# GpSimd's order inside a tile step: the low part of x behind h instead of in front of the class gather

## The chip, the core and the metric

The kernel runs on one core of a Trainium2 chip. The metric is the device time of one execution in microseconds (us), the median of several runs. The engines have names of their own here: PE is TensorE, ACT is ScalarE, DVE is VectorE, POOL is GpSimd, SP is SyncE, which issues transfers.

## What is computed

The input x has 2 batches of 2048 tokens with 512 features. A first layer adds a low-rank product with a decoded weight of each batch (rank 30). The second layer, whose cost rules the kernel, builds six variants of each token and runs an MLP with a layer norm over them:

```
x = x + x @ weight[b] + bias[b]                      # rank 30
h = ln(ln(x, pw_g[path], pw_b[path]), cp_g[comp], cp_b[comp])
t = ln(x, tm_g[comp], tm_b[comp]);   s = ln(x, ms_g[scale], ms_b[scale])
m, n, r = x + mlp_ln(state_k)                        # one vector each per batch
cat = [w0*h, w1*t, w2*m, w3*n, w4*r, w5*s]
x = x + ln(silu(cat @ W1 + b1) @ W2 + b2, g, be)
```

The products of cat that hold x itself are folded into one weight block, so that a tile needs four products of depth 512 in the first matmul (x, t, s, h) and one in the second.

## The kernel before

**Tiles and stages.** The 4096 tokens are 32 tiles of 128 tokens, tile number s. All engines run the same software pipeline: in step n, tile a = n+2 is loaded and embedded, f = n+1 gets its norms, m = n runs the first matmul, c = n-1 the second and b = n-2 the output norm. The order on every engine is written out by hand in a function `step(n)` of that engine; engines meet only at semaphores. Steps 15 to 26 are in a hardware loop of three rounds with four steps each (`steps`, `Fori`), the others are unrolled.

**Split operands.** Each float32 operand of a big product is split into a high part (fp32r) and a low part, and a product is three matmuls per chunk: high times high (L707), high times low (L708) and low times high (L709). 12 such matmuls of 128x512 make one product. For x the high part is made on ACT (`x_high`, L526) and the low part on POOL (`x_low`, L1034). For t, s, h and z the high part is ACT's copy (L555) and the low part a DVE subtraction that reads a PSUM bank (`split_lo`, L1210).

**Parked steps.** For tiles 2 to 13 the product with x was already computed in the preamble and parked in SBUF (`stash`). `kept(n)` says so: steps 2 to 13 have no x product, the other steps do ("unparked": 1 and 14 to 31). Only the unparked steps with a tile a to load, n = 1 and n = 14 to 29, are touched by the change.

**The chain of tile f on POOL and its neighbours.** In step n, PE's `expand(f)` (L768) ends with x1 on DVE (`first_sum`, L1242), then its statistics; POOL's `rstd(0, f)` turns them into rs and nm (L985, L993, L998); ACT makes xhat (`x_norm`, L604). From xhat, DVE makes st = xhat*sgt (`scale_rows`, L1262, needs the gather of sgt) and tt = xhat*ctt (`scaled`, L1254), then the low part of z of tile c (`z_split`, L1210 into zop), on which PE's `second_product(c)` (first matmul L707 that reads zop) waits, and then `out_scaled` (L1330). POOL makes h1 from xhat with two instructions (`h_first`: multiply L1043, add L1045; they need the gather of pwt). DVE takes its statistics (`h_stats`, L1215), POOL does `rstd(2, b)` and `rstd(1, f)`, ACT ht (`h_norm`, L611), DVE ht*ctt (`h_gain`, L1271) and then the low part of t (`t_split`); PE transposes ht at the start of the next step (`transpose_h`, L701) and then runs `t_product`.

**Gathers.** POOL issues three indirect transfers per tile a: ctt (`gather_class`, in the middle of the step; it also waits for tile a's indices and for `h_ready` of the tile whose slot it takes), and sgt and pwt (`gather_rest`, behind `rstd(1, f)`), all at L1010. The low part x_lo(a) is needed by PE's `embed(a)` (L758) near the end of the step and by the x product of the step n+2. The raw x of tile a comes by SP's queue (`load_x`), issued when PE has finished with the same slot.

Of the kernel before, what the change touches and what calls it, by code (L numbers as in the profile page):

```python
# [106 lines left out]
def kept(t):  # L107

    return t.i is None and PRE0 <= t.s < PRE0 + NPRE
# [13 lines left out]
def build(nc, d, out):  # L123
# [11 lines left out]
    with ExitStack() as ctx:  # L135
# [835 lines left out]
        def _(pool):  # L971
# [9 lines left out]
            def rstd(which, t, have, done):  # L981

                pool.wait_ge(have, t.count())
                pool.nop(nofuse=True)
                nc.gpsimd.tensor_scalar(ve[:, which:which + 1], mv[:, which, 1:2], EPS, 1.0, ALU.add, ALU.mult) \  # L985
                    .then_inc(pool_part, 1)
                parts[0] += 1
                pool.wait_ge(pool_part, part_count(t))
                if which == 2:
                    nc.gpsimd.tensor_tensor(rs[:, which:which + 1], ve[:, which:which + 1], mhalf[:, :],  # L990
                                            ALU.pow).then_inc(done, 1)
                    return
                nc.gpsimd.tensor_tensor(rs[:, which:which + 1], ve[:, which:which + 1], mhalf[:, :],  # L993
                                        ALU.pow).then_inc(pool_part, 1)
                parts[0] += 1
                pool.wait_ge(pool_part, part_count(t))
                pool.nop(nofuse=True)
                nc.gpsimd.tensor_scalar(nm[:, which:which + 1], mv[:, which, 0:1], rs[:, which:which + 1], -1.0,  # L998
                                        ALU.mult, ALU.mult).then_inc(done, 1)
# [14 lines left out]
            def gather_class(a):  # L1014
                s, old = a.slot, a.plus(-2)

                pool.wait_ge(idx_in[s], a.slot_count(16))
                if old.exists():
                    pool.wait_ge(h_ready, old.count())
                pool.nop(nofuse=True)  # L1020
                gather(a, ctt, "ct", 1, ct_in)

            def gather_rest(a):
                gather(a, sgt, "ms_g", 2, sg_in)
                gather(a, pwt, "pw", 0, pw_in)
# [5 lines left out]
            def x_low(a):  # L1031
                s = a.slot
                pool.wait_ge(x_hi, a.count())
                nc.gpsimd.tensor_tensor(xop[:, s, LO, :, :], xraw[s][:, :, :], xop[:, s, HI, :, :].bitcast(F32),  # L1034
                                        ALU.subtract).then_inc(x_lo, 1)

            def h_first(f):
                s = f.slot
                pool.wait_ge(xhat_ready, f.count())
                pool.wait_ge(pw_in[s], f.slot_count(16))  # L1040
                if f.plus(-1).exists():
                    pool.wait_ge(hn_ready, f.count(extra=0))
                nc.gpsimd.tensor_tensor(h1[:, :], xhat[:, :], pwt[:, s, 0:D], ALU.mult).then_inc(h1_part, 1)  # L1043
                pool.wait_ge(h1_part, f.count())
                nc.gpsimd.tensor_tensor(h1[:, :], h1[:, :], pwt[:, s, D:2 * D], ALU.add).then_inc(h1_ready, 1)  # L1045

            def residual(f):
                old = f.plus(-UNROLL)
                if old.exists():
                    pool.wait_ge(stored[f.row], old.row_count(16))  # L1050
                if is_first(f):
                    pool.wait_ge(bebc_in, 16)
                pool.wait_ge(x1_ready, f.count())
                nc.gpsimd.tensor_tensor(xb[:, f.row, :], x1[:, f.slot, :], bebc[:, :], ALU.add).then_inc(xb_ready, 1)  # L1054
# [23 lines left out]
            def step(n):  # L1078
                a, f, m, c, b = n.plus(2), n.plus(1), n, n.plus(-1), n.plus(-2)
                if f.exists():  # L1080
                    rstd(0, f, mv1_ready, r1_ready)
                if a.exists() and not kept(n):
                    x_low(a)
                if kept(n):
                    x_low(a)
                if a.exists():
                    gather_class(a)
                if f.exists():
                    h_first(f)
                if b.exists():  # L1090
                    rstd(2, b, mv3_ready, r3_ready)
                if f.exists():
                    rstd(1, f, mv2_ready, r2_ready)
                if a.exists():
                    gather_rest(a)
                if f.exists():
                    residual(f)

            first_step()
            for n in range(1, FIRST):  # L1100
                step(Tile(n))
            with pool.Fori(0, (LAST - FIRST) // UNROLL) as i:
                before = parts[0]
                base[:] = [20, i]
                for n in range(FIRST, FIRST + UNROLL):
                    step(Tile(n, i))
                assert parts[0] - before == 20
            parts[0] = before + 20 * ((LAST - FIRST) // UNROLL)
            base[1] = None
            for n in range(LAST, TILES):  # L1110
                step(Tile(n))
# [449 lines left out]
```

## Time and profile before

| what | value |
|---|---|
| time, median of 3 runs | 637.97 us (635.06 to 638.03) |
| the profiled execution's own time | 637.78 us |
| its span from first to last instruction | 636.0 us |
| busy: PE, PEld | 593.4 us, 453.1 us |
| busy: DVE, POOL, ACT | 407.6 us, 389.3 us, 204.9 us |
| mean granted TensorE clock | 0.992 of full speed |

The span is what the trace covers; the time adds 1.8 us around it. PEld is the weight load, which overlaps the matmul. A busy share is an average over stages with different limits, so it does not say by itself what a change in one stage does.

### The profile page before, as it was taken

The page shows a single profiled execution, that of the slowest core. Times are in us where ns is not written, and L with a number is a line of the kernel's source. Part 1 is how long each engine was busy: PE and PEld are TensorE (multiplying, and loading weights), DVE is VectorE, ACT ScalarE, POOL GpSimd, SP SyncE. Part 2 cuts the span into 40 slices and gives each one's busy share as a digit, 9 for nine tenths or more (in the row PEclk, how much of TensorE's full clock was granted, in tenths as well). Part 3 has the DMA queues.
Part 4 walks back from the last instruction along what each step waited for, and adds up shares of the span by engine and source line. Part 5 has one row for each costly group of instructions (what it writes and reads, how often), then busy time and mean ns, then how long its engine had stood idle before and what let it go on. Part 6 is the DMA issues. An engine that isn't in the chain of part 4 may idle for free.

```text
span 636.0 us, 9140 instructions
## 1 busy us (share of the span) xinstructions
PE 593.4 (93%) x2924; PEld 453.1 (71%) x2924; DVE 407.6 (64%) x749; ACT 204.9 (32%) x346; POOL 389.3 (61%) x499
## 2 busy tenths in 40 slices
PE   0899788989999999999999999999999999999995
PEld 0464245567878888888888777777888888787784
DVE  3411157658888888888865566556666565766655
ACT  3333235232333433334323323222333223323222
POOL 1013226666888888888856666676676676765820
PEclk9999799999999999999999999999999999999998
DMA  8999957513555445445524434444534344444301
GB/s 291 404 403 366 384 194 256 155 54 102 169 152 163 150 139 167 137 141 170 149 102 125 129 113 136 138 113 107 145 125 124 117 119 136 136 121 120 99 18 49
DMA packets 53119, 102.07 MB, mean 160 GB/s; under 512 B 10446, under 2 KB 23246, under 8 KB 52956
## 3 DMA queue, kind: packets, MB, share of 16 engines
q1 hardware_dynamic: 39872, 58.52, 27.0%
q0 software_dynamic: 12160, 42.04, 23.2%
q10 hardware_dynamic: 1052, 1.07, 0.5%
q8 instruction: 18, 0.29, 0.2%
q14 instruction: 17, 0.14, 0.1%
HBM read 93.10 MB, written 8.39 MB: 160 GB/s over the span
## 4 chain that ended last, share of the span: by engine, by line
PE 35%; POOL 16%; issue 12%; DVE 8%; DMA 8%; ACT 2%; POOLq 0%; DVEq 0%
PE bank L707 10%; PE bank L708 9%; PE bank L709 9%; DMA pwt<-in_pw,idx 7%; POOL h L1045 4%; PE bank L701 4%; POOL h L1043 3%; DVE bn L1215 3%; POOL rs L993 2%; POOL ctt L1010 2%; POOL ve L985 2%; POOL nm L998 1%; ACT ht L611 1%; DMA sgt<-in_ms_g,idx 1%; DVE x L1242 1%
## 5 line engine op out<-in xcount | busy, mean ns | idle before, releaser
L707 PE MATMUL bank<-W,ops 128*128 128x512 f32 x432 | 178.9, 414 | 1.3 <-DVE ops L1210 0.4
L708 PE MATMUL bank<-W,ops 128*128 128x512 f32 x432 | 171.3, 397 | 0.0
L709 PE MATMUL bank<-W,ops 128*128 128x512 f32 x432 | 171.0, 396 | 0.0
L707 PEld LDWEIGHTS bank<-W,ops 128*128 128x128 f32 x432 | 81.7, 189 | 29.7 <-issue 9.7
L555 ACT ACTIVATE ops<-bank 128x512 fp32r<-128x512 f32 x97 | 56.9, 589 | 136.8 <-PE bank L701 136.8
L709 PEld LDWEIGHTS bank<-W,ops 128*128 128x128 f32 x432 | 81.6, 189 | 20.0
L708 PEld LDWEIGHTS bank<-W,ops 128*128 128x128 f32 x432 | 81.9, 190 | 14.8
L1034 POOL TENSOR_TENSOR xop<-xraw,xop 128x512 fp32r<-128x512 f32 x32 | 41.8, 1307 | 65.9 <-ACT xop L526 65.8
L1210 DVE TENSOR_TENSOR ops<-bank,ops 128x512 fp32r<-128x512 f32 x97 | 66.2, 684 | 11.2 <-ACT ops L555 11.0
L1215 DVE BATCH_NORM_STATS2 bn<-h 128x6 f32<-128x512 f32 x32 | 22.2, 692 | 73.9 <-POOL h L1045 73.8
L985 POOL TENSOR_SCALAR ve<-mv 128x1 f32<-128x1 f32 x94 | 31.5, 336 | 39.5 <-DVE mv L1219 35.9
L604 ACT ACTIVATE xhat<-x,nm,rs 128x512 f32<-128x512 f32 x32 | 26.1, 815 | 83.7 <-POOL nm L998 83.7
L707 PE MATMUL bank<-W,zop 128*128 128x512 f32 x124 | 49.9, 402 | 2.1 <-DVE zop L1210 1.8
L1045 POOL TENSOR_TENSOR h<-h,pwt 128x512 f32<-128x512 f32 x32 | 48.4, 1513 | 2.5
L611 ACT ACTIVATE ht<-h,nm,rs 128x512 f32<-128x512 f32 x32 | 26.1, 815 | 73.5 <-POOL nm L998 73.5
L708 PE MATMUL bank<-W,zop 128*128 128x512 f32 x124 | 49.0, 395 | 0.0
L709 PE MATMUL bank<-W,zop 128*128 128x512 f32 x124 | 48.9, 394 | 0.0
L1010 POOL DMA_INDIRECT ctt<-in_ct,idx x32 | 37.8, 1181 | 15.9 <-DMA idx<-in_idx 8.0
L1043 POOL TENSOR_TENSOR h<-xhat,pwt 128x512 f32<-128x512 f32 x32 | 42.2, 1320 | 2.8 <-ACT xhat L604 1.2
L1054 POOL TENSOR_TENSOR xb<-x,bebc 128x512 f32<-128x512 f32 x32 | 42.1, 1317 | 0.6
L695 PE MATMUL bank<-ring,cst 128*32 128x480 f32 x128 | 19.0, 684 | 24.5 <-DMA ring<-in_W_dec 24.5
L1010 POOL DMA_INDIRECT sgt<-in_ms_g,idx x32 | 34.1, 1066 | 11.2 <-issue 11.2
(143 smaller groups left out, 1058.4 us busy)
## 6 DMA issues: line engine op xcount, KB each, us to landing
ring<-in_W_dec SPq DMA_DIRECT2D x16, 960.0 KB, 12.1
xraw<-in_xT SPq DMA_DIRECT2D x32, 256.0 KB, 4.8
x<-in_x SPq DMA_DIRECT2D x32, 256.0 KB
out<-xb SPq DMA_DIRECT2D x31, 256.0 KB, 2.0
ring<-in_int_W SPq DMA_DIRECT2D x4, 1024.0 KB, 13.4
mnr<-in_int_W SPq DMA_DIRECT2D x12, 256.0 KB, 8.2
stash<-in_xT SPq DMA_DIRECT2D x12, 256.0 KB, 12.1
idxrep<-in_rows SPq DMA_DIRECT2D x64, 32.0 KB, 4.8
```

The source lines that it names most:

```text
L555: nc.scalar.activation(dst.rearrange("p c t -> p (c t)"), bank[:, :], ACT.Copy).then_inc(done, 1)
L707: nc.tensor.matmul(bank[:, :], op[:, HI, c, :], w[:, HI, c, :], start=start and c == 0, stop=False)
L708: nc.tensor.matmul(bank[:, :], op[:, HI, c, :], w[:, LO, c, :], start=False, stop=False)
L709: last = nc.tensor.matmul(bank[:, :], op[:, LO, c, :], w[:, HI, c, :], start=False, stop=stop and c == KC - 1)
L985: nc.gpsimd.tensor_scalar(ve[:, which:which + 1], mv[:, which, 1:2], EPS, 1.0, ALU.add, ALU.mult) \
L1010: pool.indirect_dma_start(out=dst[:, s, :], out_offset=None, in_=d[table], in_offset=bass.IndirectOffsetOnAxis(ap=idx[:, s, col:col + 1], ...
L1034: nc.gpsimd.tensor_tensor(xop[:, s, LO, :, :], xraw[s][:, :, :], xop[:, s, HI, :, :].bitcast(F32), ALU.subtract).then_inc(x_lo, 1)
L1043: nc.gpsimd.tensor_tensor(h1[:, :], xhat[:, :], pwt[:, s, 0:D], ALU.mult).then_inc(h1_part, 1)
L1045: nc.gpsimd.tensor_tensor(h1[:, :], h1[:, :], pwt[:, s, D:2 * D], ALU.add).then_inc(h1_ready, 1)
L1054: nc.gpsimd.tensor_tensor(xb[:, f.row, :], x1[:, f.slot, :], bebc[:, :], ALU.add).then_inc(xb_ready, 1)
L1210: nc.vector.tensor_tensor(dst.rearrange("p c t -> p (c t)"), bank[:, :], hi.bitcast(F32).rearrange("p c t -> p (c t)"), ALU.subtract).then ...
L1215: nc.vector.bn_stats(bn[:, which, :], src).then_inc(bn_done, 1)
```

## The change

In POOL's `step(n)` the call `x_low(a)` of unparked steps stands behind `h_first(f)` instead of in front of `gather_class(a)`. Parked steps keep their order. Nothing else is touched; PE, DVE, ACT and SP have the same instructions in the same order.

```diff
                 if f.exists():
                     rstd(0, f, mv1_ready, r1_ready)
-                if a.exists() and not kept(n):
-                    x_low(a)
                 if kept(n):
                     x_low(a)
                 if a.exists():
                     gather_class(a)
                 if f.exists():
                     h_first(f)
+                if a.exists() and not kept(n):
+                    x_low(a)
                 if b.exists():
                     rstd(2, b, mv3_ready, r3_ready)
```

POOL's rows in step 1, the first unparked one, from the end of `rstd(0, f)` to the statistics of h. Before:

```order
48 L1034 TENSOR_TENSOR xop<-xraw_77,xop 128x512
49 L1010 DMA ctt<-in_ct,idx 128x1024
50 L1043 TENSOR_TENSOR h_90<-xhat,pwt 128x512
51 L1045 TENSOR_TENSOR h_90<-h_90,pwt 128x512
52 L985 TENSOR_SCALAR ve<-mv 128x1
```

And of the changed kernel:

```order
48 L1010 DMA ctt<-in_ct,idx 128x1024
49 L1043 TENSOR_TENSOR h_90<-xhat,pwt 128x512
50 L1045 TENSOR_TENSOR h_90<-h_90,pwt 128x512
51 L1034 TENSOR_TENSOR xop<-xraw_77,xop 128x512
52 L985 TENSOR_SCALAR ve<-mv 128x1
```

The subtraction into xop moved past one gather and two instructions of h; the row behind it is where it was.

In the hardware loop, POOL's rows of the first step of a round, with the semaphores that each waits for. Before:

```order
262 L998 TENSOR_SCALAR nm_97<-mv_94,rs_96 128x1 [waits pool_part]
263 L1033 REGISTER_ALU
264 L1034 TENSOR_TENSOR xop_75<-xraw1_77,xop_75 128x512 [waits x_hi]
265 L1017 ISA
266 L1019 REGISTER_ALU [waits idx_in1]
267 L1010 DMA ctt_81<-in_ct,idx_73 128x1024 [waits h_ready]
268 L1043 TENSOR_TENSOR h1_90<-xhat_87,pwt_83 128x512 [waits hn_ready,pw_in0,xhat_ready]
269 L1045 TENSOR_TENSOR h1_90<-h1_90,pwt_83 128x512 [waits h1_part]
```

And of the changed kernel:

```order
262 L998 TENSOR_SCALAR nm_97<-mv_94,rs_96 128x1 [waits pool_part]
263 L1017 ISA
264 L1019 REGISTER_ALU [waits idx_in1]
265 L1010 DMA ctt_81<-in_ct,idx_73 128x1024 [waits h_ready]
266 L1043 TENSOR_TENSOR h1_90<-xhat_87,pwt_83 128x512 [waits hn_ready,pw_in0,xhat_ready]
267 L1045 TENSOR_TENSOR h1_90<-h1_90,pwt_83 128x512 [waits h1_part]
268 L1033 REGISTER_ALU
269 L1034 TENSOR_TENSOR xop_75<-xraw1_77,xop_75 128x512 [waits x_hi]
```

The wait for x_hi, which stood ahead of gather and h, now stands behind both.

## Rows read from the trace of the kernel before

**Rows 1.** Step windows, expand to expand: length, each engine's busy us, clock, DMA.
```profile
319.05:335.96 16.91, 16.91 (x84) 13.93 (x83) 12.09 (x22) 5.71 (x10) 10.32 (x14) 1.00 0.33 112
...
405.84:423.89 18.05, 17.20 (x84) 13.84 (x83) 10.07 (x20) 4.79 (x9) 11.09 (x15) 1.00 0.39 114
...
sum 276.57, PE 274.30 PEld 222.09 DVE 173.93 ACT 82.29 POOL 183.36; mean PE 17.14 PEld 13.88 DVE 10.87 ACT 5.14 POOL 11.46
```

**Rows 2.** Waits from 319 to 606 us: us in total, times, longest.
```profile
POOL xop L1034 <- ACT xop L526: 54.5, 16, 4.7
...
DVE st L1262 <- DMA sgt<-in_ms_g,idx: 9.1, 7, 1.9
...
PEld bank L707 <- DVE zop L1210: 3.4, 5, 1.0
...
PEld bank L701 <- DVE ht L1271: 2.1, 5, 0.6
```

**Rows 3.** Timeline of a long step (expand at 405.84): start, us, instruction, [idle before].
```profile
411.77 0.69 DVE L1262 TENSOR_TENSOR st<-xhat,sgt 128x512 f32<-128x512 f32 x1 [1.90 <-DMA sgt<-in_ms_g,idx]
...
413.80 0.49 PE L707 MATMUL bank<-W,zop 128*128 128x512 f32 x1 [0.85 <-DVE zop L1210]
...
414.33 1.29 POOL L1034 TENSOR_TENSOR xop<-xraw,xop 128x512 fp32r<-128x512 f32 x1 [4.73 <-ACT xop L526]
...
418.20 1.29 POOL L1045 TENSOR_TENSOR h<-h,pwt 128x512 f32<-128x512 f32 x1
...
422.77 1.05 POOL L1010 DMA_INDIRECT sgt<-in_ms_g,idx  x1 [0.33 <-issue]
```

**Rows 4.** Timeline of a short step (expand at 319.05).
```profile
319.49 0.69 DVE L1242 TENSOR_TENSOR x<-bank,x 128x512 f32<-128x512 f32 x1 [2.66 <-PE bank L768]
...
322.37 0.26 POOL L998 TENSOR_SCALAR nm<-mv,rs 128x1 f32<-128x1 f32 x1 [0.18 <-POOL rs L993]
...
324.12 0.69 DVE L1254 TENSOR_TENSOR tt<-xhat,ctt 128x512 f32<-128x512 f32 x1
...
325.08 1.29 POOL L1034 TENSOR_TENSOR xop<-xraw,xop 128x512 fp32r<-128x512 f32 x1 [2.45 <-ACT xop L526]
...
325.99 0.39 PE L707 MATMUL bank<-W,zop 128*128 128x512 f32 x1
...
329.90 0.40 PE L758 MATMUL bank<-xop,Ust 128*128 128x256 f32 x2
```

**Rows 5.** Transfers issued from 319 to 590 us: KB each, median us to landing.
```profile
pwt<-in_pw,idx POOLq DMA_INDIRECT x15, 6.5
```

**Rows 6.** Timeline of the preamble: a class gather right behind rstd.
```profile
91.94 0.27 POOL L998 TENSOR_SCALAR nm<-mv,rs 128x1 f32<-128x1 f32 x1 [0.18 <-POOL rs L993]
...
92.67 1.07 POOL L1010 DMA_INDIRECT ctt<-in_ct,idx  x1 [0.46 <-issue]
```

**Rows 7.** Timeline of step 30 (expand at 595.62), which has no x_low and no gather.
```profile
596.70 0.68 DVE L1242 TENSOR_TENSOR x<-bank,x 128x512 f32<-128x512 f32 x1
...
600.71 0.69 DVE L1262 TENSOR_TENSOR st<-xhat,sgt 128x512 f32<-128x512 f32 x1 [0.69 <-ACT xhat L604]
601.00 1.55 POOL L1043 TENSOR_TENSOR h<-xhat,pwt 128x512 f32<-128x512 f32 x1 [1.17 <-ACT xhat L604]
...
601.32 1.78 DVE L1254 TENSOR_TENSOR tt<-xhat,ctt 128x512 f32<-128x512 f32 x1
...
603.75 0.50 PE L707 MATMUL bank<-W,zop 128*128 128x512 f32 x1 [0.60 <-DVE zop L1210]
```

**Rows 8.** Timeline at 516 us: POOL asks 0.16 us after DVE.
```profile
516.25 0.74 DVE L1330 SCALAR_TENSOR_TENSOR o<-o,mv,gbc 128x512 f32<-128x512 f32 x1
516.41 1.74 POOL L1034 TENSOR_TENSOR xop<-xraw,xop 128x512 fp32r<-128x512 f32 x1 [2.85 <-ACT xop L526]
```

**Rows 9.** Timeline of the first step of a loop round (expand at 475.76).
```profile
479.25 0.26 POOL L998 TENSOR_SCALAR nm<-mv,rs 128x1 f32<-128x1 f32 x1 [0.18 <-POOL rs L993]
...
481.25 0.68 DVE L1254 TENSOR_TENSOR tt<-xhat,ctt 128x512 f32<-128x512 f32 x1
```

## The prediction

> **What bounds the kernel now.** I read the windows of the 16 unparked steps 14 to 29 first, each from one `expand` on PE to the next. The reader is to see that a step is as long as PE is busy in the short one (16.91 of 16.91 us), while the longest takes 18.05 with PE busy for 17.20, and that the 16 sum to 276.57 [rows 1]. The clock is full. So 16.9 us is PE's own work, and 276.57 - 16 x 16.9 = 6.2 us is PE late in small pieces. Nothing else in these steps can be won, whatever moves on POOL.
>
> Then the chain of waits, for what PE stands still for: the low part of z (zop) and ht [rows 2]. Behind them stand DVE's wait for the gather of sgt, 9.1 us in 7 steps, and POOL's wait for x_hi in front of `x_low`, 54.5 us in all 16 [rows 2].
>
> Last the timeline of a long step. `x_low` starts at 414.33 after POOL has stood idle for 4.73 us, because the raw x lands late and ACT's copy with it; h ends at 419.49 and sgt's gather goes out at 422.77, 16.9 us after the step's expand [rows 3]. In the short step that idle time is only 2.45 us [rows 4]. Late gathers are felt one step on: sgt kept DVE waiting 1.90 us here and PE 0.85 us [rows 3]. It is a ring: late gathers crowd the raw x, which makes `x_low`, h and the next gathers late.
>
> **The change, part by part.** No instruction is added or removed. In steps 14 to 29 the order after `rstd(0)` was x_low, ctt, multiply, add; now it is ctt, multiply, add, x_low. I count times from the step's `expand`, with the short step as the pattern: x1 starts at 0.44, `rstd(0)` ends at 3.58, tt starts at 5.07, PE's first matmul of `second_product` at 6.94, `embed` at 10.85 [rows 4]. st ends 0.08 after tt starts [rows 7], at 5.15.
>
> *Gather.* Behind rstd a class gather started 0.46 us after nm and took 1.07 us [rows 6]. So it runs 4.04 to 5.11, and the multiply can start at 5.15 (0.04 us behind the gather, as in every step). It asks for pwt: issued at about 14.3 of the step before (below) and with a median of 6.5 us to landing [rows 5], that is 20.8 - 16.9 = 3.9, in time.
>
> *h and x_low.* If DVE keeps its pace, tt, 0.69 us long, holds the multiply up until 5.76 - 0.14: a POOL instruction that waits for a DVE one goes on 0.14 us before that one's end (the multiply behind st ended at 602.55, which is 601.40 - 0.14 + 1.29) [rows 7]. Multiply ends at 6.9. `out_scaled` (0.74 us [rows 8]) goes between, and the add ends at 8.6. `x_low` follows, 1.29 us long [rows 4], from 8.7 to 10.0, now after x_hi in nearly every step, so its wait for x_hi is gone. `embed` at 10.85 asks for it: 0.85 us to spare. Cover gone, each later us would be a us of the step.
>
> *What comes earlier.* From h's end to sgt's issue it was 3.28 us, with both rstd between [rows 3]; 0.25 of it was a wait for the statistics of h, which are now done before. So sgt goes out at 10.0 + 3.0 = 13.0 and pwt (1.05 us and 0.3 of issue later) at 14.3, where sgt went out at 16.9 in the long step [rows 3]. So the sgt wait of DVE disappears, and ht and the low part of t, which hang on the same `rstd(1)`, come 2 to 4 us earlier, more than PE ever waited for them. All the pieces of the 6.2 us go. The ctt gather goes out 4 to 6 us earlier and has the raw x beside it only at its end; I cost that at nothing, since ACT's copy of the raw x now has until 8.7 where it was needed at 6.0 [rows 4].
>
> *Step 30* starts x1 1.08 us after its expand, held up by late ht and t splits [rows 7], against 0.44 [rows 4]. So its zop and PE come 0.64 us earlier. Together 6.8 us.
>
> *The price.* h now runs beside st and tt. Rows 7 are that case: the multiply asks at 601.00, while st runs; when st ends, POOL goes first, and tt takes 1.78 us in place of 0.69. The trace shows one waiting for the other for a whole instruction: tt ends at multiply's end - 0.14 + 0.69. PE then starts zop's product late. PE starts 0.65 us behind tt's end [rows 7]. For a short step: st ends at 5.15, multiply at 5.15 - 0.14 + 1.29 = 6.30, tt at 6.85, PE at 7.50 in place of 6.94: **0.56 us** per step. Who is first decides. Where POOL asked 0.16 us after DVE had begun, DVE went first and POOL took 1.74 us [rows 8]. In an ordinary step the multiply asks at 5.15 and tt begins at 5.07, so DVE is first by 0.08 us and the price is 0. In the first step of each loop round (three of them: 15, 19, 23) tt begins 1.74 us behind rstd's end [rows 9] and the multiply asks 0.46 + 1.07 + 0.04 = 1.57 behind it: POOL is first. There tt would begin at 5.49, 0.42 later than in the pattern, so PE starts at 7.92: 0.98 us, three times 2.9 us.
>
> The bounds of that price: 0 where DVE is first everywhere; 13 x 0.56 + 2.9 = 10.2 us where POOL is first everywhere. I take DVE first in ordinary steps, by 0.08 us, which is thin: with a gather 0.33 us behind nm, as sgt's is [rows 3], it would turn.
>
> On who waits, the Trainium skill (SBUF — State Buffer, "A bandwidth-pool intuition that's wrong") says of GpSimd and a two-port instruction of VectorE that "one fully blocks"; GPSIMD Engine Reference, "Specifications", counts VectorE instructions with two SBUF inputs among those that contend. The trace agrees: tt 1.78 us in place of 0.69 [rows 7]. By the rule alone, without the order of asking, every step would pay, and the sum would be that of the second case below.
>
> *Step 1* changes too: h of tile 2 comes some 2 us earlier, but DVE is in long weight splits then; 0, within 1 us either way.
>
> **The sum.** 637.78 (the profiled execution, 0.2 under the median) - 6.8 + 2.9 = **633.9 us**, 0.6% faster.
>
> **Rivals.**
> 1. *No stall at all* (DVE first in the loop's first steps too): 637.78 - 6.8 = 631.0. For it: the margin there is 0.17 us, and the instructions between nm and the gather may take longer in the loop. Chance 0.13.
> 2. *POOL first everywhere; slower.* Then 6.8 is won and 10.2 paid: 641.2 us. It decides where the multiply asks before 5.07, that is, where the gather starts less than 0.38 us behind nm. For it: sgt starts 0.33 behind nm [rows 3]. Against it: 0.46 in the only sample of ctt [rows 6], and one more semaphore is waited for here. Chance 0.23.
> 3. *Mixed:* the winner changes from step to step, half of the 13 steps pay: 637.6. Also where some of the late landings stay, since the transfers' crowd only moves. Chance 0.14.
> 4. *x_low becomes late for embed.* Its wait replaces the one removed. It begins where h ends after 9.4, so with pwt landing after 6. With sgt issued at 13.0 it would need 8.6 us to land, against a median of 6.5 [rows 5]. Price, if it lasts at 0.3 us over: 16 x 0.3 = 4.8, with the rest 638.7; at 0.6 us over 643.5. Chance 0.07.
> My own case, DVE first but in the loop's first steps, has 0.43.
>
> **How the numbers follow.** The likeliest case gives 633.9; its own range is 632.5 to 635.5. Case 1 lies below, 2 and 3 above. From 630.5 to 641.5 lie all but case 4's upper part and the tails. A measurement here tells about 0.5% (3.2 us) from no change. Faster by more than that, under 634.8: case 1 and most of my own, 0.50. Slower, over 641.2: half of case 2 and half of case 4 with tails, 0.17. Between: 0.33.
>
> **What would show it.** Right: step windows of 16.9 us outside the loop's first steps and 17.9 in these; no wait of DVE for sgt; no wait of PE for ht; sgt issued near 13 us after expand; `x_low` ending about 10.0, `embed` not waiting; L1254 0.69 us long in ordinary steps and the multiply 1.7 to 1.8. If L1254 takes 1.78 in ordinary steps and the windows are 17.5, case 2 holds. The prediction is wrong in its base if windows stay uneven with sgt landing late, or if PE waits for xop before `embed`.

## The result, and the profile after

The change makes the kernel slower: 657.49 us (656.43 to 657.99, 6 runs) against 638.00 us of the kernel before (6 runs), ratio 1.0307, 95% interval 1.0283 to 1.0332. The forecast was 633.9 us with a range of 630.5 to 641.5.

The profiled execution took 657.37 us, 655.6 of it span. The windows from expand to expand, as in [rows 1], of the changed kernel: length, busy us of each engine, granted clock, DMA share, GB/s. The last row is steps 14 to 29 in one.

```profile
320.41:338.15 17.74, 17.20 (x85) 13.85 (x84) 12.89 (x22) 5.72 (x10) 12.20 (x15) 1.00 0.42 129
338.15:359.49 21.34, 18.73 (x84) 15.05 (x83) 14.92 (x21) 5.06 (x9) 12.40 (x15) 0.92 0.41 123
359.49:377.29 17.80, 17.20 (x84) 13.86 (x83) 12.34 (x21) 5.20 (x9) 12.07 (x15) 1.00 0.35 94
412.99:434.31 21.32, 18.73 (x84) 14.98 (x83) 14.91 (x21) 5.06 (x9) 12.40 (x15) 0.92 0.44 125
487.80:509.09 21.29, 18.70 (x84) 14.97 (x83) 14.92 (x21) 5.06 (x9) 12.40 (x15) 0.92 0.38 121
320.41:615.81 295.40, 279.80 (x1329) 225.11 (x1328) 205.34 (x337) 81.95 (x145) 195.46 (x240) 0.98 0.39 118
```

The 16 steps take 295.40 us where they took 276.57 [rows 1]: 18.8 of the 19.6 us between the two spans. The unevenness is gone, as forecast, but the ordinary steps are equally long at 17.7 to 17.9, not 16.9, and the first step of each loop round takes 21.3. The waits between 319 and 625 us (us in total, times, longest) show where PE stands:

```profile
DVE ops L1210 <- ACT ops L555: 17.7, 16, 3.0
PE bank L707 <- DVE zop L1210: 16.0, 17, 2.6
PEld bank L707 <- DVE zop L1210: 14.3, 14, 1.1
```

The waits for sgt and for ht of [rows 2] no longer stand among them; the one for zop has grown. The timeline of an ordinary step (expand at 359.49), on POOL, DVE and PE:

```profile
362.80 0.26 POOL L998 TENSOR_SCALAR nm<-mv,rs 128x1 f32<-128x1 f32 x1 [0.18 <-POOL rs L993]
...
363.61 1.03 POOL L1010 DMA_INDIRECT ctt<-in_ct,idx  x1 [0.54 <-issue]
...
363.94 0.69 DVE L1262 TENSOR_TENSOR st<-xhat,sgt 128x512 f32<-128x512 f32 x1 [0.69 <-ACT xhat L604]
364.55 1.98 DVE L1254 TENSOR_TENSOR tt<-xhat,ctt 128x512 f32<-128x512 f32 x1
364.67 1.30 POOL L1043 TENSOR_TENSOR h<-xhat,pwt 128x512 f32<-128x512 f32 x1
...
367.18 0.50 PE L707 MATMUL bank<-W,zop 128*128 128x512 f32 x1 [0.60 <-DVE zop L1210]
```

Gather and multiply start where they were put: 4.12 and 5.18 us behind expand (forecast 4.04 and 5.15); tt begins at 5.06. But tt takes 1.98 us and ends at 7.04, while the multiply, recorded 0.12 us behind it, takes 1.30, as if alone. PE starts zop's product at 7.69 in place of 6.94 [rows 4]. And the first step of a round (expand at 338.15):

```profile
342.52 1.03 POOL L1010 DMA_INDIRECT ctt<-in_ct,idx  x1 [0.61 <-issue]
...
343.04 2.41 DVE L1262 TENSOR_TENSOR st<-xhat,sgt 128x512 f32<-128x512 f32 x1 [0.84 <-ACT xhat L604]
...
343.59 1.30 POOL L1043 TENSOR_TENSOR h<-xhat,pwt 128x512 f32<-128x512 f32 x1
...
344.96 1.60 POOL L1045 TENSOR_TENSOR h<-h,pwt 128x512 f32<-128x512 f32 x1
345.37 1.74 DVE L1254 TENSOR_TENSOR tt<-xhat,ctt 128x512 f32<-128x512 f32 x1
...
347.84 0.79 PE L707 MATMUL bank<-W,zop 128*128 128x512 f32 x1 [2.61 <-DVE zop L1210]
```

Here st itself takes 2.41 us, though it begins 0.55 us before the multiply; then tt loses against the add. PE stands still for 2.61 us, and behind that the granted clock falls to half for 3.4 us of the step, in each of the three. The windows of the stall, of the stretch behind it and of the next 3.7 us show it (the clock is the third number from the end):

```profile
345.24:347.84 2.60, 0.00 (x0) 0.00 (x1) 2.60 (x4) 0.00 (x0) 2.60 (x2) 1.00 0.27 109
347.84:351.28 3.44, 3.44 (x8) 2.76 (x9) 3.03 (x5) 0.00 (x0) 2.23 (x5) 0.50 0.02 5
351.28:355.00 3.72, 3.72 (x23) 3.21 (x23) 0.97 (x3) 1.54 (x3) 2.84 (x5) 1.00 0.52 166
```

### The profile page after: what moved, and what is told of

The parts are those of the page before. It is cut to its first block, busy times and chain, and to the rows that moved or that the text cites. A ratio compares the mean times of both kernels' runs of the same rounds, so it can differ in the third digit from the quotient of the medians.

```text
span 655.6 us, 9140 instructions
## 1 busy us (share of the span) xinstructions
PE 600.4 (92%) x2924; PEld 458.3 (70%) x2924; DVE 439.2 (67%) x749; ACT 204.2 (31%) x346; POOL 396.4 (60%) x499
## 4 chain that ended last, share of the span: by engine, by line
PE 58%; DVE 13%; issue 4%; ACT 3%; POOL 3%; POOLq 0%; DVEq 0%; ACTq 0%
PE bank L707 16%; PE bank L708 15%; PE bank L709 15%; PE bank L701 6%; DVE tt L1254 5%; ACT xhat L604 2%; DVE bn L1215 2%; PE bank L758 2%; DVE x L1242 2%; POOL rs L993 2%; DVE zop L1210 2%; PE bank L777 1%; PE bank L768 1%; POOL nm L998 1%; POOL ve L985 1%
## 5 line engine op out<-in xcount | busy, mean ns | idle before, releaser
L985 POOL TENSOR_SCALAR ve<-mv 128x1 f32<-128x1 f32 x94 | 26.5, 281 | 98.9 <-DVE mv L1219 94.0
L707 PE MATMUL bank<-W,zop 128*128 128x512 f32 x124 | 52.8, 426 | 16.0 <-DVE zop L1210 16.0
L1034 POOL TENSOR_TENSOR xop<-xraw,xop 128x512 fp32r<-128x512 f32 x32 | 48.5, 1515 | 11.0 <-ACT xop L526 10.9
L1242 DVE TENSOR_TENSOR x<-bank,x 128x512 f32<-128x512 f32 x32 | 22.0, 688 | 47.5 <-PE bank L768 47.5
L1045 POOL TENSOR_TENSOR h<-h,pwt 128x512 f32<-128x512 f32 x32 | 51.1, 1598 | 2.5
L708 PE MATMUL bank<-W,zop 128*128 128x512 f32 x124 | 50.8, 410 | 0.0
L709 PE MATMUL bank<-W,zop 128*128 128x512 f32 x124 | 50.7, 409 | 0.0
L1254 DVE TENSOR_TENSOR tt<-xhat,ctt 128x512 f32<-128x512 f32 x32 | 43.5, 1360 | 2.3 <-ACT xhat L604 2.3
L707 PEld LDWEIGHTS bank<-W,zop 128*128 128x128 f32 x124 | 24.5, 197 | 29.3 <-DVE zop L1210 14.5
L993 POOL TENSOR_TENSOR rs<-ve,mhalf 128x1 f32<-128x1 f32 x64 | 40.2, 629 | 5.5 <-POOL ve L985 0.2
```

Of the source, the lines that this page charges most:

```text
L707: nc.tensor.matmul(bank[:, :], op[:, HI, c, :], w[:, HI, c, :], start=start and c == 0, stop=False)
L708: nc.tensor.matmul(bank[:, :], op[:, HI, c, :], w[:, LO, c, :], start=False, stop=False)
L709: last = nc.tensor.matmul(bank[:, :], op[:, LO, c, :], w[:, HI, c, :], start=False, stop=stop and c == KC - 1)
L1254: nc.vector.tensor_tensor(tt[:, :], xhat[:, :], ctt[:, s, D:2 * D], ALU.mult).then_inc(t_ready, 1)
```

## The experiments

Two theories. **P**: h's multiply on GpSimd takes the SBUF access that st and tt on DVE need; the low part of z is late, and PE waits. **T**: the class gather, 3.4 to 5.9 us earlier, hurts by its transfers. Each run is compared with the kernel before on the same chip. That one's median was 638.12 us (25 runs) for four of them (h held until tt, the early gather alone, the gather behind h, the low part of z first) and 637.69 us (23 runs) for the other four.

**Hold h back until tt is done.** In `h_first` of the changed kernel:

```diff
+                if f.s >= 15:
+                    pool.wait_ge(t_ready, f.count())
                 nc.gpsimd.tensor_tensor(h1[:, :], xhat[:, :], pwt[:, s, 0:D], ALU.mult)
```

> The changed kernel, but from step 14 on h's multiply also waits for tt (t_ready), so that it can't come between st and tt. Theory P (GpSimd's multiply takes the SBUF access that tt needs, so the low part of z and PE's second product are late): tt takes 0.69 us again, PE does not wait for zop, ordinary steps take 16.9 us, the whole about 631 us. Rival T (the class gather, 4 to 6 us earlier, hurts by its transfers): nothing of that kind changes, 655 us or more. In the first steps of the loop's rounds, where st took 2.4 us: if the multiply queued behind the gather is what blocks st, st takes 0.69 us and the step 16.9; if the gather itself blocks it, st takes about 1.2 us and the step over 17.2.

632.77 us, ratio 0.992 (0.9889 to 0.995): 0.8% faster than the kernel before, 3.8% than the changed one. One window over the 16 steps, and the first step of a round (expand at 404.56; two lines more in the file, so st is L1264, tt L1256 and the multiply L1045):

```profile
319.91:590.75 270.84, 270.84 (x1329) 222.59 (x1328) 183.36 (x337) 83.16 (x145) 185.63 (x240) 1.00 0.42 127
```

```profile
408.93 1.02 POOL L1010 DMA_INDIRECT ctt<-in_ct,idx  x1 [0.60 <-issue]
409.46 0.69 DVE L1264 TENSOR_TENSOR st<-xhat,sgt 128x512 f32<-128x512 f32 x1 [0.86 <-ACT xhat L604]
410.07 0.69 DVE L1256 TENSOR_TENSOR tt<-xhat,ctt 128x512 f32<-128x512 f32 x1
...
410.94 1.29 POOL L1045 TENSOR_TENSOR h<-xhat,pwt 128x512 f32<-128x512 f32 x1 [0.98 <-DVE tt L1256]
```

PE is busy for all 270.84 us, 16.93 a step. P holds, T falls: the gather is as early as in the changed kernel and costs nothing. In the first step of the round the gather started 0.60 us behind nm and st 0.53 behind the gather, just as in the slow one, and st takes 0.69 us. So it is not the gather that keeps st out, but the multiply queued behind it.

**Hold h back until st is done.** The same line with `s_ready`.

> The changed kernel, but h's multiply waits for st (s_ready) and not for tt: it can ask only once st is done and tt has begun. If an instruction that has the access keeps it, tt takes 0.69 us, the multiply about 1.6, steps 16.9, and the whole is as with the wait for tt, 632 to 633 us. If GpSimd goes first whenever it asks, tt takes 1.8 us or more and the whole 645 us or more.

632.84 us, ratio 0.9919 (0.989 to 0.9948). The multiply now asks 0.26 us behind tt's start and waits itself (expand at 355.03):

```profile
360.11 0.68 DVE L1256 TENSOR_TENSOR tt<-xhat,ctt 128x512 f32<-128x512 f32 x1
360.37 1.58 POOL L1045 TENSOR_TENSOR h<-xhat,pwt 128x512 f32<-128x512 f32 x1 [0.19 <-DVE st L1264]
```

So GpSimd does not go first whenever it asks; whoever has the access keeps it for the instruction. With 0.12 us behind tt and its waits met during the gather the multiply was first, with 0.26 and a wait met only at st's end it was second.

**The early gather alone.**

```diff
                 if a.exists():
                     gather_class(a)
+                if a.exists() and not kept(n):
+                    x_low(a)
                 if f.exists():
                     h_first(f)
-                if a.exists() and not kept(n):
-                    x_low(a)
```

> The class gather is in front, but x_low stays ahead of h: order gather, x_low, h. P: st and tt have nothing beside them, since x_low waits for the high part of x; L1254 0.69 us; time that of the kernel before, 638 us within 3. T: the early gather alone costs, 645 us or more.

633.12 us, ratio 0.9913 (0.9885 to 0.9941). Better than either theory had it: T is refuted a second time, but the 638 us given for P failed too, since that figure left out what the earlier gather wins. The same window, and the first step of a round (expand at 405.25):

```profile
320.60:591.46 270.86, 270.86 (x1330) 222.57 (x1329) 183.51 (x337) 82.06 (x145) 189.77 (x240) 1.00 0.42 127
```

```profile
409.62 1.02 POOL L1010 DMA_INDIRECT ctt<-in_ct,idx  x1 [0.60 <-issue]
410.15 0.69 DVE L1262 TENSOR_TENSOR st<-xhat,sgt 128x512 f32<-128x512 f32 x1 [0.86 <-ACT xhat L604]
...
411.61 1.29 POOL L1034 TENSOR_TENSOR xop<-xraw,xop 128x512 fp32r<-128x512 f32 x1 [0.96 <-ACT xop L526]
```

All that could be won in these steps comes from moving the gather ahead of `x_low`'s wait; that h also moved brought nothing. Behind the gather now stands an instruction whose wait (x_hi) is not yet met, and st passes with the same 0.53 us distance. POOL's wait in front of `x_low` is at most 1.3 us, where it was up to 4.7 [rows 2].

**The gather behind h.**

```diff
-                if a.exists():
+                if a.exists() and kept(n):
                     gather_class(a)
                 if f.exists():
                     h_first(f)
                 if a.exists() and not kept(n):
+                    gather_class(a)
                     x_low(a)
```

> The class gather behind h too: order rstd, h, gather, x_low. P, as step 30 of the kernel before: the multiply asks while st runs, tt takes 1.8 us, PE starts zop's product 0.56 us late and loses 0.7 us a step in all, also in the first steps of the rounds (1.0 to 1.3 there), 642 to 644 us. If only the gather makes the trouble (T, or a gather that holds the access itself): 631 to 638 us.

645.30 us, ratio 1.0111 (1.0078 to 1.0144), 1.3 us over the expected 642 to 644. An ordinary step (expand at 355.87; st is L1263, tt L1255):

```profile
360.32 0.69 DVE L1263 TENSOR_TENSOR st<-xhat,sgt 128x512 f32<-128x512 f32 x1 [0.70 <-ACT xhat L604]
360.38 1.80 POOL L1043 TENSOR_TENSOR h<-xhat,pwt 128x512 f32<-128x512 f32 x1 [0.93 <-ACT xhat L604]
360.93 1.79 DVE L1255 TENSOR_TENSOR tt<-xhat,ctt 128x512 f32<-128x512 f32 x1
...
363.38 0.50 PE L707 MATMUL bank<-W,zop 128*128 128x512 f32 x1 [0.42 <-DVE zop L1211]
```

This is the case that the forecast had computed from step 30: PE at 7.51 (7.50 computed), and at 8.02 in the first steps of the rounds (7.92). The steps take 17.6 to 17.8 and 18.1 us. So the delay of PE computed for "GpSimd asks during st" was right; the changed kernel has another case. In the first step of a round (expand at 337.74, xhat ends at 342.52) DVE is first here too:

```profile
342.64 0.69 DVE L1263 TENSOR_TENSOR st<-xhat,sgt 128x512 f32<-128x512 f32 x1 [0.85 <-ACT xhat L604]
342.76 1.72 POOL L1043 TENSOR_TENSOR h<-xhat,pwt 128x512 f32<-128x512 f32 x1 [1.25 <-ACT xhat L604]
```

st begins 0.12 us behind xhat's end, as in the changed kernel, and takes 0.69; there, with the multiply behind the gather, it took 2.41.

**The first steps of the rounds as before.** In these x_low stands in front of the gather again, else the changed order.

```diff
+                head = n.i is not None and n.s == FIRST
+                if head:
+                    x_low(a)
                 if a.exists():
                     gather_class(a)
                 if f.exists():
                     h_first(f)
-                if a.exists() and not kept(n):
+                if a.exists() and not kept(n) and not head:
                     x_low(a)
```

> The changed order, but in the first step of each of the loop's three rounds x_low stays in front of the gather. P: only the 4.4 us that each of these steps lost come back (stall of PE for zop, and a stretch at half clock behind it); the 13 others keep 17.8 us: 657.5 - 3 x 4.3 = about 644.5 us. The clock stays at full level from the preamble to the tail. If the clock falls for another reason, half-clock stretches remain in the loop and the time is over 647 us.

641.59 us, ratio 1.0064 (1.0041 to 1.0087), 3 us less than expected. The windows of steps 14 to 17:

```profile
318.78:336.52 17.74, 17.20 (x84) 13.84 (x83) 12.87 (x22) 5.72 (x10) 12.23 (x15) 1.00 0.41 130
336.52:353.52 17.00, 17.00 (x85) 13.85 (x84) 11.33 (x21) 5.06 (x9) 10.07 (x14) 1.00 0.34 106
353.52:370.42 16.90, 16.90 (x84) 13.93 (x83) 11.59 (x22) 5.21 (x9) 12.86 (x17) 1.00 0.53 140
370.42:388.30 17.88, 17.19 (x85) 13.85 (x83) 12.26 (x21) 5.07 (x9) 12.68 (x16) 1.00 0.46 133
```

The 4.3 us of each first step are back, and the clock stays full through the loop. The step behind it has the new order and yet takes 16.90, which explains the 3 us (three times 0.9 is 2.7). Its timeline says why:

```profile
357.63 1.02 POOL L1010 DMA_INDIRECT ctt<-in_ct,idx  x1 [0.54 <-issue]
358.13 0.69 DVE L1265 TENSOR_TENSOR st<-xhat,sgt 128x512 f32<-128x512 f32 x1 [0.87 <-DMA sgt<-in_ms_g,idx]
358.74 0.68 DVE L1257 TENSOR_TENSOR tt<-xhat,ctt 128x512 f32<-128x512 f32 x1
...
359.71 1.29 POOL L1043 TENSOR_TENSOR h<-xhat,pwt 128x512 f32<-128x512 f32 x1 [1.05 <-issue]
```

The gathers of the step before went out late (old order), so the multiply starts 1.06 us behind the class gather's end, past tt. The profile names no releaser, but the gather of pwt that it needs went out at 352.95 and took 6.6 us to landing, that is until 359.6. Again st begins 0.50 us behind the gather and passes.

**The low part of z first.** On DVE, `z_split(c)` ahead of `scale_rows(f)` and `scaled(f)` in unparked steps, with the changed order on POOL.

```diff
-                if f.exists():
+                if f.exists() and kept(n):
                     scale_rows(f)
                     scaled(f)
                 z_split(c)
+                if f.exists() and not kept(n):
+                    scale_rows(f)
+                    scaled(f)
                 out_scaled(b)
```

> The changed kernel, with DVE's z_split ahead of st and tt in unparked steps. P: tt (and st in the first steps of a round) still take 1.9 to 2.4 us, but the low part of z no longer waits behind them; PE does not wait for zop, steps 16.9 to 17.0, the whole 631 to 633 us. T: 655 us or more.

649.39 us (4 runs), ratio 1.0154 (1.0101 to 1.0207): the expectation failed. PE's wait for zop is gone, but another has come, in the waits from 319 to 620 us:

```profile
PEld bank L701 <- issue: 17.9, 16, 1.3
PE bank L701 <- DVE ops L1210: 14.6, 16, 1.1
```

st took 1.4 to 1.5 and tt 1.8 us, and `out_scaled` behind them as much again, so that `h_split` of tile m ended too late for `transpose_s`, which overwrites its bank. Of the 25 us that the lost access costs (657.5 against 632.8), the reordering saves 8; the rest is lost some 4 us further down the step.

**Step 1 alone.** The changed order in step 1, the old one elsewhere.

```diff
+                if a.exists() and not kept(n) and n.s > 1:
+                    x_low(a)
                 if a.exists():
                     gather_class(a)
                 if f.exists():
                     h_first(f)
-                if a.exists() and not kept(n):
+                if a.exists() and n.s == 1:
                     x_low(a)
```

> x_low behind h in step 1 alone, the other steps as before. All theories: 638 us within 1.5, since embed of tile 3 does not wait for x_low and DVE's long weight split takes up what moves. Over 640 us would mean that part of the loss lies in the preamble.

638.04 us, ratio 1.0005 (0.9983 to 1.0027): no cost of step 1 can be seen.

**A faster version.** The order gather, x_low, h, and a wait for tt ahead of the last tile's h only.

```diff
+                if is_last(f):
+                    pool.wait_ge(t_ready, f.count())
                 nc.gpsimd.tensor_tensor(h1[:, :], xhat[:, :], pwt[:, s, 0:D], ALU.mult)
...
-                if f.exists():
-                    h_first(f)
                 if a.exists() and not kept(n):
                     x_low(a)
+                if f.exists():
+                    h_first(f)
```

> Order gather, x_low, h, and only the last tile's h waits for tt. As the run with this order, whose step 30 still had tt at 1.79 us and PE 0.57 late: 0.6 us less, 632.5 us; no rival says anything else, it is the candidate for a faster version.

631.96 us, ratio 0.9913 (0.9882 to 0.9944), as expected. Faster than both kernels by 6 and 25 us; from the three other versions whose steps take 16.9 us (632.77, 632.84 and 633.12) it can't be told apart. In step 30 the trace shows what the added wait does: tt takes 0.69 us and PE starts zop's product at 6.94, where the early gather alone had 1.79 and 7.51.

## Why the prediction was wrong

- **What bounds the kernel, and the gain: right.** 276.57 - 16 x 16.9 = 6.2 us was to be had, plus 0.64 in step 30. The runs without a stall show it: 16 steps in 270.84 us, 5.7 less than before (I had taken 16.90 as the floor; it is 16.93 over all, since the first steps of a round need 17.0), and 632 to 633 us in all. In step 30 x1 starts 0.43 us behind expand, where it was 1.08, and zop's product at 7.51, where it was 8.13. The forecast's 631.0 us for no stall at all describes these runs, a third of a per cent low.
- **x_low and embed: right.** In the changed kernel x_low, 1.7 us long, ended by 10.1 us behind expand, and embed never waited for it.
- **When gather and multiply start: right within 0.2 us.** In ordinary steps the gather started at 4.04 to 4.21 (forecast 4.04) and the multiply at 5.11 to 5.27 (5.15); in the first steps of the rounds the multiply came 1.68 us behind rstd's end (1.57). sgt went out at 12.8 to 13.2 in ordinary steps (13.0 forecast), at 14.3 in the first ones.
- **Who is first: the step that failed.** "In an ordinary step the multiply asks at 5.15 and tt begins at 5.07, so DVE is first by 0.08 us and the price is 0." In fact GpSimd was first in every one of them: tt takes 1.91 to 1.98 us, the multiply 1.30. Two things were taken for granted there. A recorded start of a DVE instruction right behind another is not yet its hold on SBUF (tt is recorded 0.04 to 0.12 us before the multiply and loses). And a multiply queued behind a gather does not ask only at its own recorded start: the first steps of the rounds show this, where st began 0.55 us before it and lost. In the ordinary steps, where st ends within 0.05 us of the multiply's recorded start, either would be enough. Wherever the multiply's wait is not met during the gather (held for tt, held for st, x_low in between, pwt late) st and tt take 0.69 us with the same distances. The margin of 0.08 us was called thin; it was none.
- **The size of the price: 0.9 us a step, where the second case had 0.56.** That case had the multiply asking during st: 0.56 us a step for PE's start. Measured where that happens: 7.51, as computed. In the changed kernel the multiply starts only when the gather ends, at 5.18 in place of 5.01, so tt ends 0.19 later and PE starts at 7.69: 0.75. The steps are 0.9 longer than 16.9; another 0.15 is lost with the restart of PE's row of matmuls (the first one behind the stall is recorded with 0.50 us in place of 0.39), which was left out of the sum (in the run with the gather behind h it is 0.7 for 0.56).
- **The first steps of the rounds:** 0.98 us was computed, 4.4 measured. ACT's xhat starts 0.15 us later behind nm there, and DVE begins st 0.12 behind xhat's end where it is 0.03 otherwise; the queued multiply is first against st already, and the add against tt: 2.75 us of delay for PE (9.69 in place of 6.94). The rest, 4.4 - 2.75 = 1.65, is about what the stretch at half clock costs: 3.4 us at half speed, 1.7. That the clock could fall behind such a stall was in no case of mine.
- **The sum** with the measured terms: 637.8 - 6.8 + 13 x 0.9 + 3 x 4.4 = 655.9, 1.5 under the profiled execution. 1.4 us of this lies ahead of step 14, whose expand comes at 320.41 in place of 319.05; in the ten profiles it lies anywhere from 318.3 to 321.5, and the run with step 1 alone shows no cost there.
- **The rule of the Trainium skill** (SBUF — State Buffer, "A bandwidth-pool intuition that's wrong": "one fully blocks") was the better guide without my order of asking: the trace agrees in every ordinary step, 1.91 to 1.98 us in place of 0.69. Its plain reading gave the second case's 641.2, on the right side and still far too low.

What stays open: at what moment an instruction queued behind a gather takes the access. The runs show that its waits must be met; in the changed kernel st passed when it began 0.33 to 0.41 us behind the gather's start, and lost at 0.52 to 0.53. The distance from the gather's start need not be what counts: xhat is released to both engines at once, and where st lost it began 0.12 us behind xhat's end, elsewhere 0.03. A queued multiply that takes the access between the two would explain it as well; no run separates these. A multiply that is not queued does not do so: in the run with the gather behind h it started 0.24 us behind xhat's end in these steps, and st kept its 0.69 us.

## What to carry to other kernels

When a GpSimd tensor instruction is moved beside DVE instructions with two SBUF inputs, look for what waits behind those, and hold the GpSimd one by a semaphore rather than by a margin of a tenth of a microsecond: here the wait cost nothing that can be seen and turned +3% into -0.8%. Where several instructions move past a wait, try each alone: here the gather brought the whole gain and h the whole loss. A price computed for one stall should be followed through the tightest repeat of the pattern, here the first step of a loop round, where it was five times as large.

## What the runs showed of the hardware

- Where these GpSimd and DVE instructions met, one waited for the whole other, in both directions: tt 1.79 us in place of 0.69 behind a multiply; the multiply 1.58 in place of 1.29 behind tt, 1.80 behind st.
- A multiply queued behind an indirect gather, its waits met, kept out a DVE instruction that began 0.55 us before the multiply's recorded start (st 2.41 us). The gather alone does not: st 0.69 us at the same distance.
- After PE had stood still for 2.6 us in a row, the granted clock went from its full level of 2.4 GHz to 1.2 GHz for 3.4 us, three times out of three; stalls of 0.5 to 0.7 us in each of the other steps left it at full, and so did those of 0.9 us in the run with the gather behind h.
